# The FFN input turned by VectorE in squares of 32 instead of by TensorE, and its layer norm moved from the experts to the gates

## The chip, the cores and the metric

One Trainium2 chip, one core. The metric is the device time of the whole kernel in microseconds.

## The reference

A transformer layer over x of shape (4, 1024, 256), fp32: retention attention, then a mixture-of-experts FFN, each behind a layer norm and with a residual. The part around the change is the FFN:

```python
shared = silu(xf @ sw1 + sb1) * (xf @ sw3 + sb3) @ sw2 + sb2     # 256 -> 512 -> 256
for k in range(2):                                               # TOPK
    exp_ids = (tok * 11 + k * 7919) % 8                          # expert by the token's number
    h = gelu(x_of_expert @ w1[e] + b1[e])                        # 256 -> 256
    out[those tokens] += h @ w2[e] + b2[e]                       # 256 -> 256
y = x + (shared + out / 2) / 2                                   # xf = layernorm(x)
```

Since the expert is fixed by the token's number, no routing is computed. Tokens are sorted into 8 slots of 128 tokens per batch, and slot s is served by experts s and s-1.

## The kernel before

The attention runs over 16 parts (4 batches of 4). It writes x1, attention plus residual, to a scratch tensor in HBM. Then the FFN runs over the 4 batches. Every fp32 matrix product is made of products of a high and a low part (`x2hi`, `x2lo`; `ghi`, `glo`; `ehi`, `elo`; weights alike): ScalarE copies the high part, VectorE subtracts it to get the low part, TensorE does three matmuls.

The FFN of batch b, in the order of TensorE's program:

- `shared(b, i)`, i = 0 to 7 ("gates"): 12 matmuls of 512 columns each (L358) for h1 and h3. i below 4 is the first half of the tokens, i from 4 the second. ScalarE's `silu` makes `sil` (L753), VectorE's `gate` makes `gf` (L1035), ScalarE's `high_gate` makes `ghi` (L757), VectorE's `low_gate` makes `glo` (L1041), one gate later. The gates of batch b+1 follow the experts of batch b.
- `expert(b, q)`, q = 0 to 7: 12 matmuls of 256 columns (L358). ScalarE applies gelu into `hf`, which lies in `xres` (L768), and makes `ehi` (L772); VectorE makes `elo` (L1047, `low_expert`).
- `slot(b, s)`, s = 0 to 7: 16 matmuls (L367, L368) of the gate's and two experts' results. VectorE adds both halves of the bank to `xr` (L1053, L1055, `add_slot`). GpSimd had added the biases to all of `xr` before (L1188), once the load of `xr` landed.

TensorE's order is experts 0, 1, 2, then expert q and slot q-3 in turn, then slot 5, the transposes of the next batch, slot 6, slot 7. Each engine runs its own program in order and waits on semaphores. `slot` waits as follows, s = 0 for `elo` of the second expert, s up to 6 for `elo` of the expert after it:

```python
if s in (0, 4):
    pe.wait_ge(glo_ready, b * 8 + (s + 4))
if s >= 2:
    pe.wait_ge(o_ready, b * NE + (s - 1))
if s == 0:
    pe.wait_ge(elo_ready, b * NE + 2)
elif s < NE - 1:
    pe.wait_ge(elo_ready, b * NE + (s + 2))
```

`expert(b, 2)` waits for all eight `gf`, because it takes over a bank of the gates.

The input of the next batch, `xl`, is loaded by SyncE's queue from the scratch tensor in two halves. VectorE computes the layer norm's sums (`ln2_sums`: L1003, L1007, L1010), GpSimd raises to the power -1/2 (L1184), VectorE applies it in place (`ln2_apply`: L1015). Before, this stands in `experts` on VectorE, at q = 2 and q = 4. `transpose_x2` (L553) then turns xl with 16 transposes of 128x128 on TensorE into four banks; `high_x2` and `low_x2` make x2hi and x2lo from the banks (L743, L745, L1023, L1025). The first batch's transposes stand in the attention's last part. TensorE, VectorE, ScalarE, GpSimd and SyncE each have the first three batches in a loop (`Fori`).

Of the kernel before, what the change touches and what calls it, by code (L numbers as in the profile page):

```python
# [69 lines left out]
def moe_retention(nc, xa, xs, wattn, gnw, gnb, sw1, sw3, sw2, w1, w2, sb1, sb3, b1, sb2, b2, decay, masks, out):  # L70
# [4 lines left out]
    with ExitStack() as ctx:  # L75
        def sem(name):
            return ctx.enter_context(nc.semaphore(name))
# [87 lines left out]
        elo = [sb(f"elo{i}", [P, MR, 2 * P], F32R) for i in range(4)]  # L165

        def const(name):
            return msk[:, slice(*MASK_COLS[name])]
# [5 lines left out]
        def expert_buffer(e):  # L174
            return 3 if e == NE - 1 else e % 3
# [29 lines left out]
        ln2_stats, ln2_aggr, ln2_var, ln2_rstd, xn2_ready = (  # L205
            sem(n) for n in ("ln2_stats", "ln2_aggr", "ln2_var", "ln2_rstd", "xn2_ready"))
        t2_done, x2hi_ready, x2lo_ready = sem("t2_done"), sem("x2hi_ready"), sem("x2lo_ready")
        h1_done, h3_done, sil_ready, gf_ready, ghi_ready, glo_ready = (
# [18 lines left out]
        def _(sp):  # L227
# [106 lines left out]
            for j in range(4):  # L334
                next_xres(last, j)
            for j in range(4):
                store_x1(last, j)
            for j in range(4):
                sp.wait_ge(x1_stored[j], NBATCH * 16)
            with sp.Fori(0, last) as b:  # L340
                sp.wait_ge(t2_done, (b + 1) * 4)
                for half in range(2):
                    load_xl(b + 1, half)
                store(b, (4, 8))
                sp.wait_ge(stored, (b + 1) * 32)
                sp.dma_start(xr[:], x1_dram[b + 1]).then_inc(xr_landed, 16)
            store(last, (4, 7, 8))
            sp.wait_ge(stored, last * 32 + 48)
# [3 lines left out]
        def _(pe):  # L352
# [150 lines left out]
            def step(h):  # L503
# [9 lines left out]
                if h + 1 < PARTS:  # L513
                    project_q(h + 1)
                else:

                    transpose_x2(0, 0)
                    pe.wait_ge(pm_ready, h * PAIRS + 1)
                    output(b - 1, 2, p_bank[2])
                from_state(h)  # L520
                if h + 1 == PARTS:
                    transpose_x2(0, 1)
                    pe.wait_ge(pm_ready, h * PAIRS + 2)
                    output(b - 1, 3, p_bank[3])
                    for j in (2, 3):
                        pe.wait_ge(pm_ready, h * PAIRS + (j + 1))
                        transpose_x2(0, j)
                from_scores(h)
# [15 lines left out]

            def transpose_x2(b, j):

                half, c = j // CB, j % CB
                if j == 0 and not (isinstance(b, int) and b == 0):
                    pe.wait_ge(gelu_ready, b * NE)
                if c == 0:  # L550
                    pe.wait_ge(xn2_ready, b * 2 + (half + 1))
                for t in range(4):
                    mm = nc.tensor.transpose(t2_bank[j][:, t * P:(t + 1) * P],  # L553
                                             xl[:, 4 * half + t, c * P:(c + 1) * P], ident)
                mm.then_inc(t2_done, 1)

            def shared(b, i):
                half, m = i // MS, i % MS
                if i == 0:
                    pe.wait_ge(x2lo_ready, b * 4 + 2)  # L560
                elif i == 1:
                    pe.wait_ge(x2lo_ready, b * 4 + 4)
# [37 lines left out]

            def experts(b, more):
                for q in range(3):
                    expert(b, q)
                for q in range(3, NE):
                    expert(b, q)
                    slot(b, q - 3)
                slot(b, NE - 3)
                if more:
                    for j in range(4):
                        transpose_x2(b + 1, j)  # L610
                slot(b, NE - 2)
                slot(b, NE - 1)

# [38 lines left out]
            with pe.Fori(0, last) as b:  # L652
                experts(b, True)
                for i in range(2 * MS):
                    shared(b + 1, i)
            experts(last, False)


        @block.scalar
        def _(act):  # L660
# [79 lines left out]
            def high_x2(b, j):  # L740
                half, c = j // CB, j % CB
                act.wait_ge(t2_done, b * 4 + (j + 1))
                cp = nc.scalar.activation(x2hi[:, c, half * HALF:(half + 1) * HALF], t2_bank[j][:], ACT.Copy)  # L743
                if half == 0:
                    cp = nc.scalar.activation(x2hi[:, c, T:T + P], t2_bank[j][:, 0:P], ACT.Copy)  # L745
                cp.then_inc(x2hi_ready, 1)
# [12 lines left out]
            def experts(b, more):  # L759
                for q in range(NE):  # L760
                    e = ORDER[q]
                    act.wait_ge(e_done, b * NE + (q + 1))
                    if q >= 2:
                        act.wait_ge(elo_ready, b * NE + (q - 1))
                    if q >= 4:
                        act.wait_ge(slot_done, b * NE + (q - 2))
                    for m in range(MR):
                        ge = nc.scalar.activation(hf[q % 2][:, m, :], e_bank[q % 4][:, m * 2 * P:(m + 1) * 2 * P], ACT.Gelu,  # L768
                                                  bias=r1b[:, e, m:m + 1])
                    ge.then_inc(gelu_ready, 1)  # L770
                    act.wait_ge(gelu_ready, b * NE + (q + 1))
                    nc.scalar.activation(ehi[expert_buffer(e)][:], hf[q % 2][:], ACT.Copy).then_inc(ehi_ready, 1)  # L772
                    if q == 1:
# [45 lines left out]
        def _(dve):  # L819
# [192 lines left out]
            def ln2_apply(b, half):  # L1012
# [4 lines left out]
                ts.then_inc(xn2_ready, 1)  # L1017

            def low_x2(b, j):
                half, c = j // CB, j % CB  # L1020
                dve.wait_ge(x2hi_ready, b * 4 + (j + 1))
                at = slice(half * HALF, (half + 1) * HALF)
                tt = nc.vector.tensor_tensor(x2lo[:, c, at], t2_bank[j][:], x2hi[:, c, at].bitcast(F32), ALU.subtract)  # L1023
                if half == 0:
                    tt = nc.vector.tensor_tensor(x2lo[:, c, T:T + P], t2_bank[j][:, 0:P], x2hi[:, c, T:T + P].bitcast(F32),  # L1025
                                                 ALU.subtract)
                tt.then_inc(x2lo_ready, 1)
# [28 lines left out]

            def experts(b, more):
                low_expert(b, 0)
                low_expert(b, 1)
                low_gate(b, 2 * MS - 1)  # L1060
                for q in range(2, NE):
                    if more and q in (2, 4):
                        ln2_sums(b + 1, q // 2 - 1)
                    low_expert(b, q)
                    if more and q in (2, 4):
                        ln2_apply(b + 1, q // 2 - 1)
                    add_slot(b, q - 2)
                if more:
                    for j in range(4):
                        low_x2(b + 1, j)  # L1070
                add_slot(b, NE - 2)
                add_slot(b, NE - 1)

# [39 lines left out]
            for i in range(4, 8):  # L1113
                gate(0, i)
                low_gate(0, i - 1)
            with dve.Fori(0, last) as b:
                experts(b, True)
                for i in range(2 * MS):
                    gate(b + 1, i)
                    if i:  # L1120
                        low_gate(b + 1, i - 1)
            experts(last, False)

# [161 lines left out]
```

## Time and profile before

| | |
|---|---|
| median of 3 runs | 443.84 us (443.46 to 444.18) |
| the profiled execution | 443.61 us, its span 441.8 us |
| busy in the span: TensorE | 432.6 us, 98% |
| VectorE | 292.6 us, 66% |
| ScalarE | 216.2 us, 49% |
| GpSimd | 95.4 us, 22% |
| granted TensorE clock | 1.000 |

The span runs from the first to the last instruction of the profiled execution; the time is a little longer. Busy shares are averages over the whole span. In the profile PE is TensorE's matmul, DVE VectorE, ACT ScalarE, POOL GpSimd, SP SyncE; `bank` is any of the eight PSUM banks, since buffer numbers are left out of names.

### The profile page before, as it was taken

The page shows a single profiled execution, that of the slowest core. Times are in us where ns is not written, and L with a number is a line of the kernel's source. Part 1 is how long each engine was busy: PE and PEld are TensorE (multiplying, and loading weights), DVE is VectorE, ACT ScalarE, POOL GpSimd, SP SyncE. Part 2 cuts the span into 40 slices and gives each one's busy share as a digit, 9 for nine tenths or more (in the row PEclk, how much of TensorE's full clock was granted, in tenths as well). Part 3 has the DMA queues.
Part 4 walks back from the last instruction along what each step waited for, and adds up shares of the span by engine and source line. Part 5 has one row for each costly group of instructions (what it writes and reads, how often), then busy time and mean ns, then how long its engine had stood idle before and what let it go on. Part 6 is the DMA issues. An engine that isn't in the chain of part 4 may idle for free.

```text
span 441.8 us, 14549 instructions
## 1 busy us (share of the span) xinstructions
PE 432.6 (98%) x6318; PEld 390.7 (88%) x6318; DVE 292.6 (66%) x685; ACT 216.2 (49%) x416; POOL 95.4 (22%) x73
## 2 busy tenths in 40 slices
PE   6999999999999999999999999999999999999997
PEld 4899999999989999998989988899988999888995
DVE  5887778766876878867556654857538575575433
ACT  3466656546754476445255343472524823346430
POOL 1103323522244213540621101211004020040000
PEclk9999999999999999999999999999999999999999
DMA  7443232232321131225330005000133001120011
GB/s 259 153 141 100 98 100 74 75 100 80 123 91 51 51 125 49 88 84 189 122 119 1 18 32 200 39 0 0 47 120 117 0 0 47 47 95 0 1 47 47
DMA packets 15383, 34.64 MB, mean 78 GB/s; under 512 B 2369, under 2 KB 2657, under 8 KB 14817
## 3 DMA queue, kind: packets, MB, share of 16 engines
q1 hardware_dynamic: 14896, 33.05, 22.0%
q8 instruction: 44, 0.72, 0.7%
q10 hardware_dynamic: 432, 0.79, 0.6%
q14 instruction: 11, 0.08, 0.1%
HBM read 25.44 MB, written 8.40 MB: 77 GB/s over the span
## 4 chain that ended last, share of the span: by engine, by line
PE 80%; DVE 8%; ACT 8%; DMA 2%; issue 2%; ACTq 0%; POOL 0%; DVEq 0%
PE bank L358 44%; PE bank L367 13%; PE bank L368 7%; PE bank L437 4%; DVE pm L863 3%; PE bank L475 3%; PE bank L466 3%; ACT vexp L671 3%; ACT kexp L671 3%; DMA wqkv_raw<-wattn 2%; PE bank L553 2%; PE bank L451 2%; ACT xhi L663 1%; PE bank L416 1%; PE bank L491 1%
## 5 line engine op out<-in xcount | busy, mean ns | idle before, releaser
L768 ACT ACTIVATE xres<-bank,r1b 128x256 f32<-128x256 f32 x64 | 26.7, 469 | 54.9 <-PE bank L368 53.6
L358 PE MATMUL bank<-x2hi,sw_hi 128*128 128x512 f32 x128 | 51.2, 400 | 0.0
L753 ACT ACTIVATE sil<-bank,s1b 128x512 f32<-128x512 f32 x32 | 22.0, 688 | 58.2 <-PE bank L358 58.2
L358 PE MATMUL bank<-x2lo,sw_hi 128*128 128x512 f32 x128 | 50.4, 394 | 0.0
L358 PE MATMUL bank<-x2hi,sw_lo 128*128 128x512 f32 x128 | 50.3, 393 | 0.0
L686 ACT ACTIVATE keo<-kT,msk 128x512 f32<-128x512 f32 x32 | 21.4, 715 | 51.8 <-DVE kT L852 51.8
L367 PE MATMUL bank<-sw_both,ghi 128*128 128x512 f32 x128 | 46.5, 396 | 0.0
L367 PE MATMUL bank<-w_both,ehi 128*128 128x512 f32 x128 | 46.4, 397 | 0.0
L1035 DVE SCALAR_TENSOR_TENSOR gf<-bank,s3b,sil 128x512 f32<-128x512 f32 x32 | 23.9, 748 | 32.3 <-PE bank L358 32.3
L863 DVE TENSOR_TENSOR pm<-bank,msk 128x512 f32<-128x512 f32 x64 | 39.5, 677 | 2.5 <-PE bank L437 2.5
L358 PE MATMUL bank<-xhi,wqkv_hi 128*128 128x256 f32 x128 | 38.1, 298 | 1.3 <-DVE xlo L847 1.2
L1041 DVE TENSOR_TENSOR glo<-gf,ghi 128x512 fp32r<-128x512 f32 x32 | 35.8, 1117 | 2.6 <-ACT ghi L757 2.6
L1053 DVE TENSOR_TENSOR xr<-bank,xr 128x256 f32<-128x256 f32 x32 | 13.5, 423 | 34.8 <-PE bank L368 34.8
L358 PE MATMUL bank<-x2hi,w_lo 128*128 128x256 f32 x128 | 36.2, 283 | 0.0
L358 PE MATMUL bank<-x2lo,w_hi 128*128 128x256 f32 x128 | 36.2, 283 | 0.0
L358 PE MATMUL bank<-x2hi,w_hi 128*128 128x256 f32 x128 | 36.2, 283 | 0.0
L358 PE MATMUL bank<-xhi,wqkv_lo 128*128 128x256 f32 x128 | 36.1, 282 | 0.0
L358 PE MATMUL bank<-xlo,wqkv_hi 128*128 128x256 f32 x128 | 36.1, 282 | 0.0
L1188 POOL TENSOR_TENSOR xr<-xr,slot_bias 128x2048 f32<-128x2048 f32 x4 | 18.5, 4626 | 81.3 <-DMA xr<-x_scratch 81.3
L368 PE MATMUL bank<-sw_both,glo 128*128 128x256 f32 x128 | 35.9, 281 | 0.0
L368 PE MATMUL bank<-w_both,elo 128*128 128x256 f32 x128 | 35.9, 280 | 0.0
L1047 DVE TENSOR_TENSOR elo<-xres,ehi 128x512 fp32r<-128x512 f32 x32 | 22.1, 690 | 17.4 <-ACT ehi L772 17.4
(119 smaller groups left out, 1131.2 us busy)
## 6 DMA issues: line engine op xcount, KB each, us to landing
xin<-xa SPq DMA_DIRECT2D x16, 256.0 KB, 2.8
w_raw<-w SPq DMA_DIRECT2D x16, 256.0 KB, 3.4
xres<-xs SPq DMA_DIRECT2D x16, 256.0 KB, 3.3
x_scratch<-xres SPq DMA_DIRECT2D x16, 256.0 KB, 3.6
xl<-x_scratch SPq DMA_DIRECT2D x8, 512.0 KB, 5.1
xr<-x_scratch SPq DMA_DIRECT2D x4, 1024.0 KB, 4.9
out<-xr SPq DMA_DIRECT2D x7, 512.0 KB, 2.6
sw_raw<-sw SPq DMA_DIRECT2D x6, 256.0 KB, 4.0
```

What stands on the lines that cost most here:

```text
L358: mm = nc.tensor.matmul(o, w[c][l], x[c][r], start=first and c == 0 and j == 0, stop=last and c == n - 1 and j == 2)
L367: nc.tensor.matmul(o.rearrange("p (k d) -> p k d", k=2), hi, w[c], start=c == 0, stop=c == n - 1, skip_group_check=True)
L368: mm = nc.tensor.matmul(o[:, 0:D], lo, w[c][:, 0, :], start=False, stop=c == n - 1, skip_group_check=True)
L671: cp = nc.scalar.activation(dst[64 * h2:64 * h2 + 64, :, f, :, h2, :], src[64 * f:64 * f + 64, :, :, h2, :], ACT.Copy)
L686: cp = nc.scalar.activation(keo[:, :, :, odd, :], kT[:].rearrange("p g (c j) -> p c g j", c=CPS), ACT.Copy, scale=parity[:, odd:odd + 1])
L753: nc.scalar.activation(sil[i % 2][:], h1_bank[i % 2][:], ACT.Silu, bias=s1b[:, m:m + 1]).then_inc(sil_ready, 1)
L768: ge = nc.scalar.activation(hf[q % 2][:, m, :], e_bank[q % 4][:, m * 2 * P:(m + 1) * 2 * P], ACT.Gelu, bias=r1b[:, e, m:m + 1])
L863: nc.vector.tensor_tensor(pm[p][:], p_bank[p][:].rearrange("p (a i) -> p a i", i=CH), causal.unsqueeze(1).broadcast_to([P, CPS * GROUPS, C ...
L1035: nc.vector.scalar_tensor_tensor(gf[i % 3][:], h3_bank[i % 2][:], s3b[:, m:m + 1], sil[i % 2][:], ALU.add, ALU.mult).then_inc(gf_ready, 1)
L1041: nc.vector.tensor_tensor(glo[half][:, m, :], gf[i % 3][:], ghi[half][:, m, :].bitcast(F32), ALU.subtract).then_inc(glo_ready, 1)
L1047: nc.vector.tensor_tensor(elo[k][:], hf[q % 2][:], ehi[k][:].bitcast(F32), ALU.subtract).then_inc(elo_ready, 1)
L1188: nc.gpsimd.tensor_tensor(xr[:], xr[:], slot_bias[:], ALU.add).then_inc(biased, 1)
```

## The change

For batches 1 to 3, the turning moves from TensorE to VectorE. `turn_x2` makes 32 VectorE transposes per batch. One takes 32 partitions of xl (quadrant i) over four tiles and two channel halves and writes quadrant j of a new tensor `x2t` in SBUF, each 32x32 square turned. They are spread over `experts` in seven runs of 4, 2, 5, 5, 5, 5 and 6. `high_x2` and `low_x2` read x2t. Batch 0 keeps TensorE's transposes. The layer norm of the next batch moves from the experts to gates 4 to 7: sums, apply, sums, apply. `low_x2` and the last additions are reordered. ScalarE waits for the slot after the gelu instead of before. Gate 4 instead of gate 1 waits for the second half of x2lo. SyncE loads the first xl before the last x1 stores, and each later one after the xr load. VectorE's and SyncE's loops are written out.

```diff
@@ sync
+            sp.wait_ge(t2_done, 4)
+            for half in range(2):
+                load_xl(1, half)
             for j in range(4):
                 store_x1(last, j)
...
-            with sp.Fori(0, last) as b:
-                sp.wait_ge(t2_done, (b + 1) * 4)
-                for half in range(2):
-                    load_xl(b + 1, half)
+            for b in range(last):
                 store(b, (4, 8))
                 sp.wait_ge(stored, (b + 1) * 32)
                 sp.dma_start(xr[:], x1_dram[b + 1]).then_inc(xr_landed, 16)
+                if b + 2 < NBATCH:
+                    sp.wait_ge(x2t_ready, (b + 1) * 2)
+                    for half in range(2):
+                        load_xl(b + 2, half)
@@ tensor, shared
-                elif i == 1:
+                elif i == MS:
                     pe.wait_ge(x2lo_ready, b * 4 + 4)
@@ tensor, experts
-                slot(b, NE - 3)
-                if more:
-                    for j in range(4):
-                        transpose_x2(b + 1, j)
-                slot(b, NE - 2)
-                slot(b, NE - 1)
+                for i in range(NE - 3, NE):
+                    slot(b, i)
@@ scalar, high_x2
-                act.wait_ge(t2_done, b * 4 + (j + 1))
-                cp = nc.scalar.activation(x2hi[:, c, half * HALF:(half + 1) * HALF], t2_bank[j][:], ACT.Copy)
+                if isinstance(b, int) and b == 0:
+                    act.wait_ge(t2_done, j + 1)
+                    src = t2_bank[j][:]
+                else:
+                    act.wait_ge(x2t_ready, (b - 1) * 2 + (half + 1))
+                    src = x2t[:, c, half * HALF:(half + 1) * HALF]
+                cp = nc.scalar.activation(x2hi[:, c, half * HALF:(half + 1) * HALF], src, ACT.Copy)
@@ scalar, experts
-                    if q >= 4:
-                        act.wait_ge(slot_done, b * NE + (q - 2))
                     for m in range(MR):
                         ge = nc.scalar.activation(hf[q % 2][:, m, :], e_bank[q % 4][:, m * 2 * P:(m + 1) * 2 * P], ACT.Gelu,
                                                   bias=r1b[:, e, m:m + 1])
                     ge.then_inc(gelu_ready, 1)
                     act.wait_ge(gelu_ready, b * NE + (q + 1))
+                    if q >= 4:
+                        act.wait_ge(slot_done, b * NE + (q - 2))
@@ vector
+            def turn_x2(b, first, end):
+
+                for n in range(first, end):
+                    half, i, j = n // 16, n % 16 // 4, n % 4
+                    if n % 16 == 0:
+                        dve.wait_ge(xn2_ready, b * 2 + (half + 1))
+                    dst = x2t[32 * j:32 * j + 32, :, half * HALF:(half + 1) * HALF].rearrange("p c (t i k) -> p t c i k", i=4, k=32)
+                    src = xl[32 * i:32 * i + 32, 4 * half:4 * half + 4, :].rearrange("p t (c j k) -> p t c j k", c=CB, j=4)
+                    tr = nc.vector.transpose(dst[:, :, :, i, :], src[:, :, :, j, :])
+                    if n % 16 == 15:
+                        tr.then_inc(x2t_ready, 1)
@@ vector, experts
+                runs = itertools.pairwise((0, 4, 6, 11, 16, 21, 26, 32))
+
+                def turn():
+                    if more:
+                        turn_x2(b + 1, *next(runs))
+
+                turn()
                 low_expert(b, 0)
                 low_expert(b, 1)
                 low_gate(b, 2 * MS - 1)
-                for q in range(2, NE):
-                    if more and q in (2, 4):
-                        ln2_sums(b + 1, q // 2 - 1)
+                turn()
+                for q in range(2, NE - 1):
                     low_expert(b, q)
-                    if more and q in (2, 4):
-                        ln2_apply(b + 1, q // 2 - 1)
                     add_slot(b, q - 2)
-                if more:
-                    for j in range(4):
-                        low_x2(b + 1, j)
-                add_slot(b, NE - 2)
-                add_slot(b, NE - 1)
+                    turn()
+                low_expert(b, NE - 1)
+                add_slot(b, NE - 3)
+                for half in range(2):
+                    if more:
+                        low_x2(b + 1, 2 * half)
+                        low_x2(b + 1, 2 * half + 1)
+                    add_slot(b, NE - 2 + half)
+
+            def next_ln(b, i):
+
+                if b < last and i >= MS:
+                    (ln2_sums, ln2_apply)[i % 2](b + 1, (i - MS) // 2)
@@ vector, batches
             for i in range(4, 8):
                 gate(0, i)
                 low_gate(0, i - 1)
-            with dve.Fori(0, last) as b:
+                next_ln(0, i)
+            for b in range(last):
                 experts(b, True)
                 for i in range(2 * MS):
                     gate(b + 1, i)
                     if i:
                         low_gate(b + 1, i - 1)
+                    next_ln(b + 1, i)
             experts(last, False)
```

## Rows read from the trace of the kernel before

**Rows 1.** The page's busy times: us, share of the span, instructions.

```profile
PE 432.6 (98%) x6318; PEld 390.7 (88%) x6318; DVE 292.6 (66%) x685; ACT 216.2 (49%) x416; POOL 95.4 (22%) x73
```

**Rows 2.** Waits of TensorE's matmuls, whole span: total us, times, longest.

```profile
PE bank L620 <- DVE vexp L1075: 2.0, 1, 2.0
...
PE bank L358 <- DVE xlo L847: 1.2, 4, 0.5
```

**Rows 3.** The chain that ended last, in the FFN stage: start, us, what.

```profile
258.66 1.75 PE bank L553 x16
...
266.03 28.15 PE bank L358 x144
...
316.76 1.75 PE bank L553 x16
```

**Rows 4.** Timeline, VectorE and ScalarE, last slots of batch 0: start, us, instruction.

```profile
248.93 0.41 DVE L1053 TENSOR_TENSOR xr<-bank,xr 128x256 f32<-128x256 f32 x1
...
249.72 0.68 DVE L1047 TENSOR_TENSOR elo<-xres,ehi 128x512 fp32r<-128x512 f32 x1
...
255.89 0.42 DVE L1053 TENSOR_TENSOR xr<-bank,xr 128x256 f32<-128x256 f32 x1 [1.93 <-PE bank L368]
255.97 0.84 ACT L768 ACTIVATE xres<-bank,r1b 128x256 f32<-128x256 f32 x2 [2.74 <-PE bank L368]
...
256.84 0.63 ACT L772 ACTIVATE ehi<-xres 128x512 fp32r<-128x512 f32 x1
...
257.50 0.69 DVE L1047 TENSOR_TENSOR elo<-xres,ehi 128x512 fp32r<-128x512 f32 x1 [0.73 <-ACT ehi L772]
```

**Rows 5.** Timeline of VectorE, layer norm among the experts of batch 0.

```profile
235.99 1.40 DVE L1003 BATCH_NORM_STATS2 ln_st<-xl 128x6 f32<-128x256 f32 x4
...
238.06 0.69 DVE L1047 TENSOR_TENSOR elo<-xres,ehi 128x512 fp32r<-128x512 f32 x1
239.66 1.39 DVE L1015 TENSOR_SCALAR xl<-xl,ln_mv,ln_r 128x256 f32<-128x256 f32 x4 [0.91 <-POOL ln_r L1184]
240.96 0.41 DVE L1053 TENSOR_TENSOR xr<-bank,xr 128x256 f32<-128x256 f32 x1
```

**Rows 6.** Timeline of VectorE, gates and first experts of batch 1.

```profile
275.13 4.67 DVE L1041 TENSOR_TENSOR glo<-gf,ghi 128x512 fp32r<-128x512 f32 x1
279.73 0.74 DVE L1035 SCALAR_TENSOR_TENSOR gf<-bank,s3b,sil 128x512 f32<-128x512 f32 x1
280.39 0.67 DVE L1041 TENSOR_TENSOR glo<-gf,ghi 128x512 fp32r<-128x512 f32 x1
280.99 0.74 DVE L1035 SCALAR_TENSOR_TENSOR gf<-bank,s3b,sil 128x512 f32<-128x512 f32 x1
...
292.87 0.69 DVE L1047 TENSOR_TENSOR elo<-xres,ehi 128x512 fp32r<-128x512 f32 x1 [0.75 <-ACT ehi L772]
```

**Rows 7.** Timeline of TensorE, first or last matmuls of stages.

```profile
235.92 0.39 PE L367 MATMUL bank<-sw_both,ghi 128*128 128x512 f32 x1
...
258.38 0.28 PE L368 MATMUL bank<-w_both,elo 128*128 128x256 f32 x1
...
265.86 0.40 PE L358 MATMUL bank<-x2hi,sw_hi 128*128 128x512 f32 x1
...
288.26 0.28 PE L358 MATMUL bank<-x2hi,w_hi 128*128 128x256 f32 x1
...
294.01 0.39 PE L367 MATMUL bank<-sw_both,ghi 128*128 128x512 f32 x1
...
298.25 0.39 PE L367 MATMUL bank<-sw_both,ghi 128*128 128x512 f32 x1
```

**Rows 8.** Timeline of GpSimd, gates of batch 1.

```profile
274.63 4.62 POOL L1188 TENSOR_TENSOR xr<-xr,slot_bias 128x2048 f32<-128x2048 f32 x1 [27.04 <-DMA xr<-x_scratch]
```

**Rows 9.** Timeline of VectorE, gate 4 of batch 0.

```profile
222.03 0.75 DVE L1035 SCALAR_TENSOR_TENSOR gf<-bank,s3b,sil 128x512 f32<-128x512 f32 x1 [1.92 <-PE bank L358]
222.70 1.82 DVE L1041 TENSOR_TENSOR glo<-gf,ghi 128x512 fp32r<-128x512 f32 x1
```

More of the change, by code:

```diff
@@ L1 @@
+import itertools
 from contextlib import ExitStack
@@ L165, in moe_retention @@
         elo = [sb(f"elo{i}", [P, MR, 2 * P], F32R) for i in range(4)]
+        x2t = sb("x2t", [P, CB, T])
         def const(name):
@@ L206, in moe_retention @@
             sem(n) for n in ("ln2_stats", "ln2_aggr", "ln2_var", "ln2_rstd", "xn2_ready"))
+        x2t_ready = sem("x2t_ready")
         t2_done, x2hi_ready, x2lo_ready = sem("t2_done"), sem("x2hi_ready"), sem("x2lo_ready")
@@ L515, in step @@
                 else:
-                    transpose_x2(0, 0)
+                    transpose_x2(0)
                     pe.wait_ge(pm_ready, h * PAIRS + 1)
@@ L521, in step @@
                 if h + 1 == PARTS:
-                    transpose_x2(0, 1)
+                    transpose_x2(1)
                     pe.wait_ge(pm_ready, h * PAIRS + 2)
@@ L526, in step @@
                         pe.wait_ge(pm_ready, h * PAIRS + (j + 1))
-                        transpose_x2(0, j)
+                        transpose_x2(j)
                 from_scores(h)
@@ L543, in step, with transpose_x2 @@
                     scores(h + 1)
-            def transpose_x2(b, j):
+            def transpose_x2(j):
                 half, c = j // CB, j % CB
-                if j == 0 and not (isinstance(b, int) and b == 0):
-                    pe.wait_ge(gelu_ready, b * NE)
                 if c == 0:
-                    pe.wait_ge(xn2_ready, b * 2 + (half + 1))
+                    pe.wait_ge(xn2_ready, half + 1)
                 for t in range(4):
@@ L599, in slot, with experts @@
                 wide_product(o_bank[s % 2][:], g, w).then_inc(slot_done, 1)
-            def experts(b, more):
+            def experts(b):
                 for q in range(3):
@@ L652, in _ @@
             with pe.Fori(0, last) as b:
-                experts(b, True)
+                experts(b)
                 for i in range(2 * MS):
                     shared(b + 1, i)
-            experts(last, False)
+            experts(last)
         @block.scalar
@@ L741, in high_x2 @@
                 half, c = j // CB, j % CB
-                act.wait_ge(t2_done, b * 4 + (j + 1))
-                cp = nc.scalar.activation(x2hi[:, c, half * HALF:(half + 1) * HALF], t2_bank[j][:], ACT.Copy)
+                if isinstance(b, int) and b == 0:
[5 more added lines that the diff above has]
+                cp = nc.scalar.activation(x2hi[:, c, half * HALF:(half + 1) * HALF], src, ACT.Copy)
                 if half == 0:
-                    cp = nc.scalar.activation(x2hi[:, c, T:T + P], t2_bank[j][:, 0:P], ACT.Copy)
+                    cp = nc.scalar.activation(x2hi[:, c, T:T + P], src[:, 0:P], ACT.Copy)
                 cp.then_inc(x2hi_ready, 1)
@@ L1022, in low_x2 @@
                 at = slice(half * HALF, (half + 1) * HALF)
-                tt = nc.vector.tensor_tensor(x2lo[:, c, at], t2_bank[j][:], x2hi[:, c, at].bitcast(F32), ALU.subtract)
+                src = t2_bank[j][:] if isinstance(b, int) and b == 0 else x2t[:, c, at]
+                tt = nc.vector.tensor_tensor(x2lo[:, c, at], src, x2hi[:, c, at].bitcast(F32), ALU.subtract)
                 if half == 0:
-                    tt = nc.vector.tensor_tensor(x2lo[:, c, T:T + P], t2_bank[j][:, 0:P], x2hi[:, c, T:T + P].bitcast(F32),
-                                                 ALU.subtract)
+                    tt = nc.vector.tensor_tensor(x2lo[:, c, T:T + P], src[:, 0:P], x2hi[:, c, T:T + P].bitcast(F32), ALU.subtract)
                 tt.then_inc(x2lo_ready, 1)
```

## The prediction

> **What bounds the kernel now.** I read the busy shares first. TensorE is busy for 98% of the span and VectorE for 66% [rows 1]; that names a candidate, no more. The list of waits, cut to TensorE, comes second: its largest wait is 2.0 us at the start, and no line of the FFN stage stands in it [rows 2]. The chain that ended last is the third: through the FFN it is matmuls without a break, such as 28.15 us of L358 in one piece, and in it stands the part that the change removes, 1.75 us of 16 transposes [rows 3]. So what TensorE no longer does comes off the time one for one, and what TensorE is made to wait comes on top one for one. The question is whether VectorE, with the turning and the moved layer norm, still delivers in time. For that the reader is to look at when each slot or gate is due on TensorE, and when VectorE's last input for it is done.
>
> **What is removed.** One row of 1.75 us stands at each of three batch ends (258.66 and 316.76 are shown, the third is alike) [rows 3]: 3 x 1.75 = 5.25 us off the path. The wait for x2lo_ready that moves from gate 1 to gate 4 is on the path nowhere today (no such row of TensorE's waits), so it gives nothing. ScalarE's wait for the slot moves behind the gelu, so ehi of the last expert can come 0.87 us earlier (256.84 becomes 255.97) [rows 4]; VectorE is then still turning, so it gives nothing either.
>
> **The price of one turn.** No row shows a VectorE transpose. Each handles 4 x 2 x 32 = 256 elements of a lane, on 32 lanes. Four operations of 256 elements in SBUF take 1.40 us together (bn_stats) or 1.39 (tensor_scalar), that is, next start 1.30 after the first, 0.33 each [rows 5]. That is the lower bound, since lanes work side by side and fewer of them save nothing. If each element took two passes it would be like a 512-element operation, 0.60 us from start to start (280.39 to 280.99) [rows 6]; that is the upper bound. I take 0.35, close to the lower one, because size per lane sets all the rows that I have and I allow a little for filling and emptying the square. Call it c. 32 turns are 11.2 us of VectorE per batch; over a batch of 58.1 us (from the transposes of one to those of the next) [rows 3] VectorE has the time as a sum. The places decide.
>
> The Trainium skill (VectorE: DVE Perf Modes, The three transpose paths) gives 311 ns for VectorE on a 128x128 array of bf16, which is 128 elements of a lane; an estimate from it for 256 elements, less 0.08 us of overlap, is c = 0.36, and the sum below would be 0.3 us higher. The same page sends a 128x128 transpose to TensorE. No run here shows it yet.
>
> **Place 1: slot 0.** Slot 0 waits for elo of the second expert. Times from the batch's first shared matmul, S = 265.86: slot 0 starts at 294.01, S+28.15, and elo of expert 1 starts at 292.87 and takes 0.69, so it is there at S+27.70 [rows 6, 7]. The cover is 0.45 us. Now add what VectorE gets between gate 4 and that point, each from issue to issue:
> - gate 3 starts late, at 279.73, because a glo took 4.67 us while GpSimd added the bias to xr for 4.62 us [rows 6, 8]. The Trainium skill (SBUF — State Buffer, Who interferes with whom) says that a VectorE instruction with two SBUF inputs and a GpSimd one that reads SBUF block each other; this trace agrees. The transfers before that addition keep their order in this stretch, so the late start stays. Gate 4 starts at 280.99, S+15.13.
> - a gate costs 0.66 and a glo 0.60; layer-norm sums 2.07 (235.99 to 238.06), and apply can't start before 3.67 after the sums began (235.99 to 239.66, GpSimd's power between) and costs 1.30 [rows 5, 6].
> - gate 4, glo, sums: 3.34. Gate 5 and glo, 1.27, would end 3.34 after the sums began, so 0.33 of waiting for the power, then apply 1.30: together 2.90. Gates 6 and 7 again: 3.34 and 2.90. Sum 12.48.
> - four turns: 4 x 0.35 = 1.40. Then elo of expert 0, 0.61, and of expert 1, 0.69 to its end: 1.30.
>
> 15.13 + 12.48 + 1.40 + 1.30 = S+30.31. Slot 0 starts 0.05 later (ehi ends at 257.47 and elo starts at 257.50, so a step between engines costs 0.03 at least [rows 4]), at S+30.36: 2.21 us late. That holds for the experts of batches 1 and 2. In batch 0, gate 4 is at 222.03, its glo is held until about 224.44, and slot 0 is at 235.92 [rows 7, 9]: 224.44 + 2.07 + 2.90 + 3.34 + 2.90 + 1.40 + 1.30 = 238.35, with 0.05 that is 2.48 late. Gate 7's result, which expert 2 waits for, is also some tenths late, but slot 0 comes after it and swallows that. Sum of place 1: 2.48 + 2 x 2.21 = 6.90 us.
>
> **Place 2: slot 6.** The last run has six turns and stands between the addition of slot 4 and elo of the last expert, and slot 6 waits for that. Today the transposes lie between slots 5 and 6 and cover it. Addition at 255.89, its pair 0.79 from issue to issue (248.93 to 249.72), six turns 2.10, elo 0.69: 259.47. TensorE is ready at 258.50, 0.12 after the last matmul of slot 5 at 258.38 [rows 4, 7]. With 0.05 that is 1.02 late, three times: 3.06 us.
>
> **Between them** each run of five turns costs 1.75. From the end of slot q-2 to elo of expert q+1 VectorE needs about 0.03 + 0.79 + 1.75 + 0.69 = 3.3 us, while slot q starts two experts and one slot later; an expert and a slot take 4.24 us (294.01 to 298.25), an expert alone a quarter of 288.26 to 294.01, 1.44 [rows 7], so 5.7 us. It holds up to c near 0.8. low_x2 and the copy of x2 stand beside two slots of 2.8 us and cost nothing; without that cover they would cost their four long and two short subtractions, some 2.8 us per batch. SP's queue: the first xl load moves ahead of the last x1 stores, which wait for later results anyway, and the others move behind the xr load and wait for turns that ended two slots before. The load of xr had landed when GpSimd began at 274.63 [rows 8]; xl is issued right behind it, and the sums want it at 280.99 + 1.26 = 282.25, 7.6 us later. Nothing there. VectorE's and SP's loops are written out; I price that at nothing, as they have idle time at the loop ends, with 1 us over three batches as its upper end.
>
> **Sum.** -5.25 + 6.90 + 3.06 = +4.7 us. The profiled execution took 443.61 us, 441.8 of them span, and the median is 443.84; I add to the median: 448.5 us. As a function of c, the waits are 2.70 + 12c in place 1 and 3 x (6c - 1.08) in place 2, if positive. With c = 0.33 the change is +4.1, with 0.60 it is +12.2 and more. It is zero at c = 0.19.
>
> **Rivals.**
> - *A turn at half the rate.* c = 0.60: 2.70 + 7.20 + 7.6 - 5.25 = +12.2, and slot 5 starts to wait too, about 1 us a batch: 458 to 459 us. Nothing in the rows speaks for it but that four-byte turns are not in them.
> - *The turn is fast and the cover holds (the other side).* One mechanism: turns of 256 elements at less than 0.19 us each. The place is the same two waits; at c = 0.10 place 2 vanishes and place 1 is 3.9, so -1.4 us, 442.5 us. It decides from c = 0.19 down. Against it: neither bn_stats nor tensor_scalar in SBUF goes below 0.33.
> - *Turns at two elements per step.* 256 elements then cost 128 steps less, c = 0.33 - 0.13 = 0.20: +0.2 us, about 444.0 us, no change that can be told. Against it: tensor_scalar on SBUF has the same 0.33 as bn_stats [rows 5], so one-input SBUF work doesn't run doubled here. The Trainium skill (VectorE: DVE Perf Modes, Mode 2×_2P) allows fp32 copies and tensor_scalar two elements per cycle; by that rule a turn might have it.
> - *The moved layer norm runs closer than I add it* (power shorter, GpSimd's addition earlier): at most 0.33 x 2 per batch and 0.9 of backlog in batches 1 and 2, 3.8 us in all: +0.9 us, 444.7. This lies on my side and is part of the lower end.
>
> **How the numbers follow.** My forecast, c of 0.33 to 0.45 with both places waiting: 0.68. Half rate: 0.10. Fast turns: 0.09. Doubled rate: 0.06. Layer norm closer: 0.07. Slower by over 0.2% (0.9 us, about what a measurement of this kernel can tell) is 0.68 + 0.10 + half of the last = 0.82; within 0.2% is 0.06 + the rest of it, with 0.01 of the fast case, = 0.10; faster 0.08. The range takes the forecast and the closer layer norm, 444.8 at the bottom, and c up to 0.45 (2.70 + 5.40 + 4.86 - 5.25 = +7.7) with the 1 us of the written-out loops and some late semaphores, 453.5 at the top.
>
> **What would show it.** In the profile after: L553 with 16 transposes instead of 64; 96 VectorE transposes, each about 0.43 us long and 0.35 apart; TensorE rows that wait for elo (slots 0 and 6), three times 2.2 to 2.5 us and three times 1.0; gates 5 to 7 late by 1 to 2 us, with no wait of TensorE for them but a small one at expert 2. If a turn takes 0.2 us, or elo of expert 1 comes before S+28.15, the prediction is wrong.

## The result, and the profile after

The changed kernel takes 450.76 us (median of 5, 449.86 to 450.94) against 443.84 (median of 5). The ratio is 1.0147, with a 95% interval of 1.0135 to 1.0159. It is 6.5 to 6.9 us slower; the forecast was 4.7 us, in a range up to 453.5.

The page's busy times and two of its costliest groups, with the idle time ahead of the group at the row's end:

```profile
PE 430.9 (96%) x6270; PEld 387.1 (86%) x6270; DVE 333.0 (74%) x781; ACT 217.8 (48%) x416; POOL 93.0 (21%) x73
...
L376 PE MATMUL bank<-sw_both,ghi 128*128 128x512 f32 x128 | 46.7, 398 | 10.2 <-DVE elo L1067 10.2
...
L1035 DVE STREAM_TRANSPOSE x2t<-xl 32x256 f32<-32x256 f32 x96 | 41.8, 435 | 1.5
```

TensorE lost 48 matmul records and 1.7 us of busy time, and its share fell from 98% to 96% [rows 1]: work went off and idle time came on. VectorE gained 96 instructions. TensorE's waits say where the idle time is. In the kernel before no such line belonged to the FFN [rows 2]:

```profile
PE bank L376 <- DVE elo L1067: 10.2, 6, 1.7
```

Six waits, and all six are the first matmul of a slot. TensorE's timeline, with the last expert or slot matmul ahead of two of them:

```profile
238.61 0.50 PE L376 MATMUL bank<-sw_both,ghi 128*128 128x512 f32 x1 [1.70 <-DVE elo L1067]
...
261.16 0.28 PE L377 MATMUL bank<-w_both,elo 128*128 128x256 f32 x1
263.15 0.47 PE L376 MATMUL bank<-sw_both,ghi 128*128 128x512 f32 x1 [1.71 <-DVE elo L1067]
...
296.85 0.28 PE L367 MATMUL bank<-x2lo,w_hi 128*128 128x256 f32 x1
298.78 0.50 PE L376 MATMUL bank<-sw_both,ghi 128*128 128x512 f32 x1 [1.64 <-DVE elo L1067]
...
323.32 0.47 PE L376 MATMUL bank<-sw_both,ghi 128*128 128x512 f32 x1 [1.71 <-DVE elo L1067]
...
359.14 0.50 PE L376 MATMUL bank<-sw_both,ghi 128*128 128x512 f32 x1 [1.70 <-DVE elo L1067]
...
383.68 0.47 PE L376 MATMUL bank<-sw_both,ghi 128*128 128x512 f32 x1 [1.71 <-DVE elo L1067]
```

They alternate: slot 0 of batches 0, 1, 2 (238.61, 298.78, 359.14) and slot 6 (263.15, 323.32, 383.68). From start to start a wait costs more than its idle time. Slot 6 was due at 261.16 + 0.12 = 261.28 and starts at 263.15, 1.87 late, and so in the other two batches: 5.6 us. Slot 0 is measured from the batch's first gate matmul. For batch 0 that is this row of the kernel before, and this one of the changed kernel; the third row is the changed kernel's for batch 1:

```profile
218.98 0.39 PE L358 MATMUL bank<-x2hi,sw_hi 128*128 128x512 f32 x1
...
219.50 0.39 PE L367 MATMUL bank<-x2hi,sw_hi 128*128 128x512 f32 x1
...
268.82 0.40 PE L367 MATMUL bank<-x2hi,sw_hi 128*128 128x512 f32 x1
```

In batch 0 slot 0 stood 16.94 us behind it [rows 7] and stands 19.11 behind it now, 2.17 late. In batches 1 and 2 it stood 28.15 behind and stands 29.96 and 30.14 behind: 1.81 and 1.99 late. That is 6.0 us. The matmul after each wait also holds up its successor by 0.06 to 0.1 us, 0.5 in all. The sum is 12.1 us, less the 5.25 of the transposes +6.8, against 6.5 to 6.9 measured. The stretch from the first gate matmul to the end of the span shows the same: 222.8 us before (218.98 to 441.8) and 229.6 after (219.50 to 449.1). The attention ahead of it, which ends between 218.3 and 220.1 in the traces, only scatters.

A smaller delay stands ahead of slot 0 in batch 0, at expert 2, which waits for all eight `gf`. The list of waits leaves it out, since most of it is a step of less than 0.15 us of idle time. Its first matmul, before and after:

```profile
233.04 0.28 PE L358 MATMUL bank<-x2hi,w_hi 128*128 128x256 f32 x1
...
233.80 0.36 PE L367 MATMUL bank<-x2hi,w_hi 128*128 128x256 f32 x1
```

From the first gate matmul that is 14.06 and 14.30, 0.24 late. The wait at slot 0 swallows it.

VectorE's timeline between gate 3 and the experts of batch 1, which answers to [rows 6]:

```profile
282.61 0.74 DVE L1055 SCALAR_TENSOR_TENSOR gf<-bank,s3b,sil 128x512 f32<-128x512 f32 x1
283.27 0.68 DVE L1061 TENSOR_TENSOR glo<-gf,ghi 128x512 fp32r<-128x512 f32 x1
283.87 0.74 DVE L1055 SCALAR_TENSOR_TENSOR gf<-bank,s3b,sil 128x512 f32<-128x512 f32 x1
284.53 0.68 DVE L1061 TENSOR_TENSOR glo<-gf,ghi 128x512 fp32r<-128x512 f32 x1
285.13 1.39 DVE L1011 BATCH_NORM_STATS2 ln_st<-xl 128x6 f32<-128x256 f32 x4
...
287.19 0.75 DVE L1055 SCALAR_TENSOR_TENSOR gf<-bank,s3b,sil 128x512 f32<-128x512 f32 x1
287.86 0.68 DVE L1061 TENSOR_TENSOR glo<-gf,ghi 128x512 fp32r<-128x512 f32 x1
288.46 1.38 DVE L1023 TENSOR_SCALAR xl<-xl,ln_mv,ln_r 128x256 f32<-128x256 f32 x4
...
294.35 1.38 DVE L1023 TENSOR_SCALAR xl<-xl,ln_mv,ln_r 128x256 f32<-128x256 f32 x4
295.64 1.77 DVE L1035 STREAM_TRANSPOSE x2t<-xl 32x256 f32<-32x256 f32 x4
297.43 1.29 DVE L1067 TENSOR_TENSOR elo<-xres,ehi 128x512 fp32r<-128x512 f32 x2
```

No row from 282.61 to 298.72 has idle time in brackets, and VectorE is busy for 15.7 of these 16.1 us: it works almost without a break and is late. The batch's first gate matmul is at S = 268.82, and elo of expert 1 ends at 298.72 = S+29.90, where slot 0 is due at S+28.15. The end of batch 0, which answers to [rows 4]:

```profile
258.67 0.42 DVE L1073 TENSOR_TENSOR xr<-bank,xr 128x256 f32<-128x256 f32 x1 [0.39 <-PE bank L377]
259.13 0.42 DVE L1075 TENSOR_TENSOR xr<-bank,xr 128x256 f32<-128x256 f32 x1
259.58 2.69 DVE L1035 STREAM_TRANSPOSE x2t<-xl 32x256 f32<-32x256 f32 x6
262.31 0.69 DVE L1067 TENSOR_TENSOR elo<-xres,ehi 128x512 fp32r<-128x512 f32 x1
```

Six turns take 2.69 us, 0.45 each, and elo is done at 263.00.

### The profile page after: what moved, and what is told of

It is laid out like the page before. It is cut to its first block, busy times and chain, and to the rows that moved or that the text cites. A ratio compares the mean times of both kernels' runs of the same rounds, so it can differ in the third digit from the quotient of the medians.

```text
span 449.1 us, 14425 instructions
## 1 busy us (share of the span) xinstructions
PE 430.9 (96%) x6270; PEld 387.1 (86%) x6270; DVE 333.0 (74%) x781; ACT 217.8 (48%) x416; POOL 93.0 (21%) x73
## 4 chain that ended last, share of the span: by engine, by line
PE 69%; DVE 20%; ACT 8%; issue 2%; DMA 1%; POOL 0%; DVEq 0%; ACTq 0%
PE bank L367 36%; PE bank L376 12%; PE bank L377 6%; DVE pm L871 3%; PE bank L446 3%; PE bank L484 3%; ACT kexp L674 3%; PE bank L475 3%; DVE x2t L1035 3%; ACT vexp L674 3%; DVE xl L1023 2%; DVE ln_st L1011 2%; DVE gf L1055 2%; DVE glo L1061 2%; PE bank L460 2%
## 5 line engine op out<-in xcount | busy, mean ns | idle before, releaser
L1035 DVE STREAM_TRANSPOSE x2t<-xl 32x256 f32<-32x256 f32 x96 | 41.8, 435 | 1.5
L376 PEld LDWEIGHTS bank<-sw_both,ghi 128*128 128x128 f32 x128 | 24.1, 188 | 16.2 <-issue 6.0
L780 ACT ACTIVATE ehi<-xres 128x512 fp32r<-128x512 f32 x32 | 20.3, 633 | 32.9 <-PE bank L377 32.4
```

The costliest lines, as they stand in the source:

```text
L376: nc.tensor.matmul(o.rearrange("p (k d) -> p k d", k=2), hi, w[c], start=c == 0, stop=c == n - 1, skip_group_check=True)
L1035: tr = nc.vector.transpose(dst[:, :, :, i, :], src[:, :, :, j, :])
```

## The experiments

**Where the time went: move the runs of turns.** Three variants of the changed kernel. In the first, the first run stands behind elo of experts 0 and 1:

```diff
-                turn()
                 low_expert(b, 0)
                 low_expert(b, 1)
                 low_gate(b, 2 * MS - 1)
+                turn()
                 turn()
```

> The changed kernel, with the first run of four turns moved behind elo of experts 0 and 1 and the last glo. Theory (TensorE waits at slot 0 and slot 6 for VectorE, and nothing else costs): elo of expert 1 comes four turns, 1.79 us, earlier; slot 0's wait shrinks from some 1.9 to 2.3 us to 0.1 to 0.5 in each of three batches; slot 6's waits stay. 450.8 - 5.3 = 445.5 us. Rival (the cost is spread: written-out loops, load order, reads of x2t, whatever the place of the turns): no change, 450.8 us.

It took 445.07 us, 1.0025 (1.0013 to 1.0036) of the kernel before. That is 5.7 us less than the changed kernel (by the medians, which are of different rounds), and TensorE's waits for elo are down to three, those of slot 6:

```profile
PE bank L376 <- DVE elo L1067: 5.1, 3, 1.7
```

In the second, the last run is moved behind the addition of slot 6, and with it the second half of `low_x2` behind the addition of slot 7:

```diff
-                    turn()
+                    if q < NE - 2:
+                        turn()
...
-                for half in range(2):
-                    if more:
-                        low_x2(b + 1, 2 * half)
-                        low_x2(b + 1, 2 * half + 1)
-                    add_slot(b, NE - 2 + half)
+                if more:
+                    low_x2(b + 1, 0)
+                    low_x2(b + 1, 1)
+                add_slot(b, NE - 2)
+                turn()
+                add_slot(b, NE - 1)
+                if more:
+                    low_x2(b + 1, 2)
+                    low_x2(b + 1, 3)
```

> The changed kernel, with the last run of six turns moved from ahead of elo of the last expert to behind the addition of slot 6. Theory: the three waits of 1.95 us at slot 6 vanish, slot 0's stay: 450.8 - 5.8 = 445.0 us; the last addition of a batch comes 0.7 us later, which may add some tenths. Rival (spread cost): no change, 450.8 us.

It took 444.19 us, 1.0011 (1.0001 to 1.0022). Again three waits are left, now those of slot 0, 4.7 us in all. The third has both edits:

> Both moves together. Theory: the waits are separate terms, so they add: 450.8 - 5.3 - 5.8 = 439.7 us, with at most 0.5 us per batch left at slot 0. Rival one (spread cost): 450.8. Rival two (the moved turns make new waits, at slot 1 for elo of expert 2, or at gate 4 for the second half of x2lo): one of the gains is lost, 445 us.

It took 439.47 us, 0.9909 (0.9887 to 0.9932). The list has no wait of TensorE for elo any more. The two gains, 5.7 and 6.6 us, sum to 12.3, and together they gave 11.3. The stretch from the first gate matmul to the end of the span, which leaves the attention's scatter out, is sharper: 229.6 us in the changed kernel, 224.2 and 223.5 with one move, 218.1 with both. The gains are 5.5 and 6.1 us, and 11.5 together: separate terms, as the theory has it. The same kernel was measured once more in five rounds.

> The kernel with both runs moved, once more in five rounds, as the standard for the next one and for a tighter interval. Theory and rivals as before: 439.5 us, 0.990 of the kernel before; if that ratio was luck of four runs, it lies at 0.995 or above.

It took 438.79 us, 0.9886 (0.9867 to 0.9905). So the turning on VectorE is a gain of 4.5 to 4.8 us, once nothing of it stands ahead of what TensorE waits for. The stretch behind the first gate matmul is 4.7 us shorter than in the kernel before (218.1 against 222.8). The half microsecond that is missing from 5.25 lies in batch 0, where expert 2 and slot 0 are still late by steps too short for the list (slot 0 stands 17.32 behind the first gate matmul, 0.38 late). With it the sum closes, so the other parts of the change cost nothing that these traces show.

**The layer norm alone.** The kernel before, with the layer norm moved to the gates as in the change, the first and later xl loads placed likewise, and both loops written out; TensorE transposes. Its edit is `next_ln` of the diff and this:

```diff
-                    if more and q in (2, 4):
-                        ln2_sums(b + 1, q // 2 - 1)
                     low_expert(b, q)
-                    if more and q in (2, 4):
-                        ln2_apply(b + 1, q // 2 - 1)
```

> The kernel before, with only the layer norm moved to gates 4 to 7 (and the loads of xl that this needs, and the loops of VectorE and SyncE written out); TensorE keeps its transposes. Theory: elo of expert 1 comes at S+28.1 against S+28.15 for slot 0, so slot 0 waits about 0.1 us in batches 1 and 2 and some 0.4 in batch 0: 443.8 + 0.6 = 444.4 us. Rival (loops written out, load order or layer norm at the gates cost by themselves): 3 us or more over the kernel before, 447 us.

It took 444.05 us, 1.0003 (0.9991 to 1.0015): none of the parts in it costs more than 0.7 us, the written-out loops included, and the rival's 3 us are out. The list has no wait of TensorE in the FFN. By starts there is a small one: slot 0 stands 17.31 us behind the first gate matmul in batch 0 (0.37 late), 28.15 in batch 1 (on time) and 28.32 in batch 2 (0.17 late), and the stretch to the end of the span is 223.6 us against 222.8. That is the 0.6 us of the expectation; the medians are too coarse for it. So the layer norm uses up the slack of slot 0 and a little more, and it is the four turns that make the long wait.

**What TensorE's transposes cost.** The kernel before, with each of them issued twice:

```diff
-                for t in range(4):
+                for t in [t for _ in range(times) for t in range(4)]:
```

> The kernel before, with each of TensorE's 48 transposes of batches 1 to 3 issued twice. It prices what the change removes. Theory: they lie on the path at 1.75 us per batch, so twice costs 5.2 us more: 449.0 us. Rival (they are partly hidden, slots 6 and 7 would wait anyway): under 2.5 us more.

It took 449.48 us against 444.26, 1.0116 (1.0081 to 1.0151): +5.2 us, and 1.75 per batch from start to start in its trace. The term of 5.25 holds from the other side as well.

Then the changed kernel with 16 transposes put back between slots 5 and 6. They turn a constant into banks that nothing reads:

```diff
-                for i in range(NE - 3, NE):
-                    slot(b, i)
+                slot(b, NE - 3)
+                if more:
+                    pe.wait_ge(gelu_ready, (b + 1) * NE)
+                    for j in range(4):
+                        for t in range(4):
+                            nc.tensor.transpose(t2_bank[j][:, t * P:(t + 1) * P], msk[:, j * 32:j * 32 + P], ident)
+                slot(b, NE - 2)
+                slot(b, NE - 1)
```

> The changed kernel, with 16 TensorE transposes of a constant put back between slots 5 and 6, into banks that nothing reads. Theory: TensorE waits there 1.95 us for elo anyway, so 1.7 us of transposes fill the wait and the time stays within 0.5 us of the changed kernel, 450.8 to 451.3 us. Rival (the transposes cost their time wherever they stand, or slot 6's wait isn't one for VectorE): 450.8 + 5.2 = 456.0 us.

It took 450.4 us, 1.0144 (1.0109 to 1.0179), the same as the changed kernel. The 5.2 us of work fit into the idle time ahead of slot 6, and the waits for elo fall from six to three. So the removal at that place bought nothing: it uncovered a wait as long as the work, and 0.2 us longer (1.95 against 1.75, with the step behind the first matmul).

**The price of a turn.** The changed kernel with pairs of VectorE operations behind its last addition:

```diff
+            measure(nc.vector.transpose, flat[0], ((32, 32), (32, 64), (32, 128), (32, 256), (32, 512)))
+            measure(nc.vector.transpose, flat[1], ((128, 128), (128, 256), (128, 512)))
+            measure(nc.vector.tensor_copy, flat[2], ((32, 256), (128, 256), (128, 512)))
```

> The changed kernel with pairs of VectorE transposes and copies behind its last addition, for their durations: 32 lanes of 32, 64, 128, 256, 512 elements, 128 lanes of 128, 256, 512; copies of 32x256, 128x256, 128x512, all fp32 in SBUF. Theory: one element of a lane per step of about 1.04 ns, the lanes for nothing, a fixed part near 0.17 us and no overlap with the next: 32x128 0.30 us, 32x256 and 128x256 both 0.435, 32x512 0.70. Rival (two passes over less fixed time): 32x512 near 0.87, twice 32x256. Copies, if doubled rate applies: 128x256 about 0.28 us instead of 0.41.

Its groups by form, busy time and mean ns of one:

```profile
L1167 DVE STREAM_TRANSPOSE xres<-xl 128x512 f32<-128x512 f32 x2 | 1.3, 657 | 0.0
L1167 DVE STREAM_TRANSPOSE x2t<-xl 32x512 f32<-32x512 f32 x2 | 1.2, 657 | 0.0
...
L1167 DVE COPY slot_bias<-xl 128x512 f32<-128x512 f32 x2 | 0.7, 408 | 0.0
L1167 DVE STREAM_TRANSPOSE xres<-xl 128x256 f32<-128x256 f32 x2 | 0.7, 391 | 0.0
L1167 DVE STREAM_TRANSPOSE x2t<-xl 32x256 f32<-32x256 f32 x2 | 0.7, 390 | 0.0
...
L1167 DVE COPY slot_bias<-xl 128x256 f32<-128x256 f32 x2 | 0.5, 274 | 0.0
L1167 DVE STREAM_TRANSPOSE x2t<-xl 32x128 f32<-32x128 f32 x2 | 0.4, 256 | 0.0
L1167 DVE STREAM_TRANSPOSE xres<-xl 128x128 f32<-128x128 f32 x2 | 0.4, 256 | 0.0
```

One element of a lane takes (657 - 390) / 256 = 1.04 ns and the fixed part is 0.12 us; 32 lanes cost what 128 do. Two passes fall, and so does the doubled rate for a transpose. The copies take (408 - 274) / 256 = 0.52 ns per element, so doubled rate there is. The Trainium skill (VectorE: DVE Perf Modes, Mode 2×_2P) allows two elements per cycle for fp32 copies and tensor_scalar. The copies agree; the kernel's tensor_scalar, at 0.406 us for 128x256, does not, and the transposes don't get it either. For the Trainium skill (VectorE: DVE Perf Modes, The three transpose paths) the nearest row is the 128x128, 0.256 us in fp32 here, where it gives 311 ns for bf16.

But the kernel's turns take 0.435, and 0.45 from start to start, not 0.39. The next run looked for the reason in the pattern of addresses, with three transposes for each of four patterns, all reading quadrant 0 and each group writing a quadrant of its own:

```diff
+            for k, (spread_dst, spread_src) in enumerate(((False, False), (False, True), (True, False), (True, True))):
+                for n in range(3):
+                    ... dst = bufs[n][32 * k:32 * k + 32, ...]; src = xl[0:32, ...]
+                    nc.vector.transpose(dst, src)
```

> The changed kernel with twelve transposes of 32x256 behind its last addition, three each: both sides contiguous; source in the kernel's pattern (rows of 32 out of 128); destination in the kernel's pattern; both. Contiguous ones took 0.39 us in the run of sizes, the kernel's 0.435. Theory: the pattern costs 0.045 us of duration, most likely the destination's, and the whole of the gap to the next start (0.45 in place of the 0.33 of other operations) is the operation's own: even contiguous ones start 0.40 apart. Rival: contiguous transposes overlap and start 0.33 apart, so the layout alone made the term too small.

Its timeline of VectorE:

```profile
446.98 0.39 DVE L1174 STREAM_TRANSPOSE slot_bias<-xl 32x256 f32<-32x256 f32 x1
447.38 0.43 DVE L1174 STREAM_TRANSPOSE x2t<-xl 32x256 f32<-32x256 f32 x1
447.75 0.39 DVE L1174 STREAM_TRANSPOSE xres<-xl 32x256 f32<-32x256 f32 x1
448.08 0.39 DVE L1174 STREAM_TRANSPOSE slot_bias<-xl 32x256 f32<-32x256 f32 x1
448.49 0.44 DVE L1174 STREAM_TRANSPOSE x2t<-xl 32x256 f32<-32x256 f32 x1
...
450.28 0.40 DVE L1174 STREAM_TRANSPOSE slot_bias<-xl 32x256 f32<-32x256 f32 x1
```

The address pattern hardly matters: contiguous or scattered, it is 0.39 or 0.44. What matters is the place in the group. Within a group, starts are 0.32 to 0.37 apart; the first of a group, which writes another quadrant, starts only when the last one has ended, and takes 0.435. (The first of each group also writes `x2t` and not another tensor, but in the run of sizes transposes into `x2t` took 0.390, so the tensor isn't the reason.) The expectation's theory was wrong in the address pattern, and its rival right in that turns can overlap. That gave a new theory, tested by sorting the turns by written quadrant:

```diff
-                    half, i, j = n // 16, n % 16 // 4, n % 4
+                    half, i, j = n // 16, n % 4, n % 16 // 4
```

> The changed kernel, with the same 32 turns sorted by the quadrant that they write (four sources in turn into quadrant 0, then into 1, and so on), where the changed kernel writes another quadrant with every turn. Theory: a turn costs 0.45 us because the next one can't start before its end when the written quadrant changes; in the run of patterns, turns to the same quadrant started 0.33 apart and those to another 0.40 and with 0.435 us of duration. So three of four now cost 0.33: the first run of four is 0.36 us shorter, the last run of six, with two changes of quadrant, about 0.4 us. Slot 0 and slot 6 wait that much less, three times: -2.3 us, 448.5 us. Rivals: the change of the quadrant that is read costs the same, and the pace stays 0.45: 450.8 us; or it is the jump within x2t from one turn to the next, which remains: 450.8 us too.

It took 449.96 us, 1.0134 (1.0113 to 1.0155), not to be told from the changed kernel's 1.0147, and six turns still take 2.70:

```profile
L1035 DVE STREAM_TRANSPOSE x2t<-xl 32x256 f32<-32x256 f32 x96 | 41.8, 436 | 1.5
...
258.52 2.70 DVE L1035 STREAM_TRANSPOSE x2t<-xl 32x256 f32<-32x256 f32 x6
```

The theory falls in that form: here the written quadrant stays for four turns and the read one changes with each. What fits all these runs is that a turn waits for the end of the operation before it when either the read or the written quadrant changes. No run was made to test it, but the trace of the changed kernel holds two checks. The first turn of a batch and the seventeenth read and write quadrant 0, behind an operation on all 128 lanes. These six alone of the 96 start before their predecessor has ended, by 0.08 (the apply at 294.35 ends at 295.73, the run starts at 295.64 by the rows above); all others start 0.01 to 0.03 after it. And in some steps both quadrants change. This is the turn from quadrant 1 to 3, and behind it the one from 2 to 0:

```profile
243.14 0.44 DVE L1035 STREAM_TRANSPOSE x2t<-xl 32x256 f32<-32x256 f32 x1
...
243.59 0.43 DVE L1035 STREAM_TRANSPOSE x2t<-xl 32x256 f32<-32x256 f32 x1
```

They are 0.45 apart too. A step such as 0 to 0, then 1 to 1, is in no run.

**Sum or place.** Half as many turns of twice the size, in runs of 3, 3, 3, 3, 3 and 1, with nothing of them ahead of elo of experts 0 and 1:

```diff
+                    dst = x2t[32 * j:32 * j + 32].rearrange("p c (t i k) -> p t c i k", i=4, k=32)
+                    src = xl[32 * i:32 * i + 32].rearrange("p t (c j k) -> p t c j k", c=CB, j=4)
...
-                runs = itertools.pairwise((0, 4, 6, 11, 16, 21, 26, 32))
+                runs = itertools.pairwise((0, 3, 6, 9, 12, 15, 16))
...
-                turn()
                 low_expert(b, 0)
```

> The changed kernel with 16 turns of 512 elements (both halves of the tokens in one) in place of 32 of 256, in runs of 3, 3, 3, 3, 3 and 1, none ahead of elo of experts 0 and 1. Theory: what counts is what stands ahead of the two dues. Nothing stands ahead of slot 0's; ahead of slot 6's one turn of 0.70 us, so elo of the last expert is ready 2.5 us after slot 4's end, when 2.6 are there: no wait there, and 439.5 us as with both runs moved, though the layout differs. If a turn of 512 in the kernel's pattern takes 0.85 us, slot 6 waits a tenth or two per batch: 440.2 us. Rival (VectorE's sum counts, not the place): 3 us of VectorE less per batch should give more than a microsecond beyond the kernel with both runs moved, 438 us or less.

It took 439.37 us, 0.9903 (0.9886 to 0.9921), against 0.9886 for both runs moved, in the same rounds. The turns are shorter in sum:

```profile
L1035 DVE STREAM_TRANSPOSE x2t<-xl 32x512 f32<-32x512 f32 x48 | 33.7, 702 | 0.9
```

8.1 us of VectorE less, and no gain; the rival's 438 us or less didn't come. As long as nothing that TensorE waits for is late, the place of the work counts and its sum doesn't.

**One more step.** Both runs moved, and the second half's apply behind the last glo too:

```diff
                 low_gate(b, 2 * MS - 1)
+                if more:
+                    ln2_apply(b + 1, 1)
...
-                if b < last and i >= MS:
+                if b < last and MS <= i < 2 * MS - 1:
```

> Both runs of turns moved, and the second half's layer norm applied behind elo of expert 1 and the last glo instead of behind gate 7. Theory: what is left of slot 0's wait (0.1 to 0.5 us per batch) goes, as 1.3 us less stands before elo of expert 1; but elo of expert 2 stands behind 1.3 us of apply and six turns, due at S+32.3 for slot 1 and ready at about S+32.2: 439 to 440.5 us. Rival: slot 1 now waits, 442 us or more.

It took 440.5 us, 0.9916 (0.9883 to 0.9949), no better than without. In its trace slot 0 is on time, but TensorE waits again, twice, 0.8 us in all, at slot 1 of batches 1 and 2. This is the first:

```profile
297.29 0.69 DVE L1067 TENSOR_TENSOR elo<-xres,ehi 128x512 fp32r<-128x512 f32 x1
...
298.04 0.50 PE L376 MATMUL bank<-sw_both,ghi 128*128 128x512 f32 x1 [0.40 <-DVE elo L1067]
```

The apply and six turns now stand ahead of elo of expert 2. From the first gate matmul to the end of the span it is 219.6 us against 218.1. The work had to go somewhere, and the next due is near.

## Why the prediction was right

- *The bound.* What TensorE is spared comes off and what it waits comes on, one for one: right. Twice the transposes cost 5.2 us. The late starts less the removed work sum to 6.8, where 6.5 to 6.9 was measured, and the variant without waits won 4.5 to 4.8 us on the kernel before.
- *Removed, 5.25 us.* Right in size. In the view of the idle-filled run, though, the three pieces of 1.75 us and the waits at slot 6 are one thing: the transposes were the cover of what came late.
- *Place 1, 6.90 us.* Right in place, and 6.0 us by starts (2.17 + 1.81 + 1.99, where I had 2.48 + 2.21 + 2.21). That it came so near is partly luck, since two errors went against each other in each batch. Four turns took 1.79 us in place of 1.40. The apply waited for nothing: it starts 3.33 us after the sums (285.13 to 288.46), where I had added 3.67 from [rows 5], 0.66 us too much in two halves. GpSimd's power takes 1.02 us there; in the kernel before it took 1.42, beside a VectorE subtraction. The small delay of expert 2 that I expected is there, 0.24 us in batch 0.
- *Place 2, 3.06 us.* This is the term that was mis-sized: 5.1 us idle, 5.6 by starts. Six turns took 2.69 in place of 2.10. They also start 0.12 later behind the addition and end 0.04 ahead of elo, since these turns overlap with neither. And 0.15 passes between the end of elo (263.00) and the matmul, where I had put 0.05. These four make up the 0.85 between 1.02 and 1.87.
- *The first matmul after a wait.* It holds up the next by 0.06 to 0.1 us, 0.5 in all. My sum had no term for it. So the forecast of +4.7 and the +6.8 of the starts differ by -0.9 in place 1, +2.6 in place 2 and this +0.5.
- *The price of a turn, 0.35.* The length that I gave one turn, 0.43, was right; what failed is the 0.08 of overlap with its neighbour. I took the rows of operations on fixed lanes as the measure, and they do give the 0.33 of turns that keep their quadrants. That a change of quadrant ends the overlap stood in no row. My bounds of 0.33 and 0.60 held it; 0.45 gives +7.7 by the formula. With the 0.66 taken off in each of three batches that is +5.7, and with the small terms of place 2 (0.26 each) and the first matmuls +7.0, close to the 6.8 of the starts.
- *The parts priced at nothing.* The load order, the written-out loops and the moved wait: the layer norm alone, with all of these but the last, came out at 1.0003, and the sum with both runs moved closes without a term for any of them.
- *The rivals.* Half rate and doubled rate fell by the sizes. Fast turns fell likewise. Against the doubled rate I had argued that one-input work in SBUF doesn't run doubled here; the copies do, so that argument was wrong and only its conclusion held. The layer norm that runs closer was half right: 0.66 us per batch, but with less than 0.1 off the backlog.

## What to carry to other kernels

When work moves from the bounding engine to one with spare time, don't ask whether the sum fits, ask what each piece stands ahead of. Here 42 us of VectorE work, with the transposes taken off TensorE, cost 6.9 us in one order and gained 4.5 to 4.8 us in another, with ten of 32 pieces per batch in another place. And a piece that is taken out of the bounding engine's program may have been the cover of a wait: look at what is due right behind it.

## What the runs showed of the hardware that I had not expected

- A VectorE transpose of 32x256 fp32 takes 0.39 us and its successor starts 0.32 to 0.37 after it when both read and both write the same quadrants. In the kernel's turns, where one of the two or both change each time, it takes 0.435 and the next starts 0.45 after.
- 32 and 128 lanes take the same time: 0.390 and 0.391 for 256 elements, 0.657 both for 512.
- An fp32 copy of 128x256 in SBUF takes 0.274 us and one of 128x512 0.408, while tensor_scalar with two operands per lane takes 0.406 for 128x256; the transpose has the slower rate of one element per 1.04 ns.
